# Eight layernorms whose centred residual is made by one product with (identity less 1/128) and read from its PSUM bank

## The reference, cut to what matters

```python
def _layernorm(x, axis=-1, eps=1e-05):
    m = jnp.mean(x, axis=axis, keepdims=True)
    v = jnp.var(x, axis=axis, keepdims=True)
    return (x - m) / jnp.sqrt(v + eps)

    x = L0_attn_x
    x = _layernorm(x + _L0_attn_ref(x, ...), axis=-1)
    x = _layernorm(x + _L0_ffn_ref(x, ...), axis=-1)
...
    x = _layernorm(x + _L3_ffn_ref(x, ...), axis=-1)
    return x
```

## Time and profile before

| | us |
|---|---|
| median of 3 runs | 3070.89 (3068.77 to 3072.56) |
| the profiled execution | 3057.68 |
| its span, first to last instruction | 3055.9 |
| delta rule with its start, 7.4 to 1361.0 | about 1354 |
| one layernorm, first product to last multiply (1361.61 to 1373.91) | 12.3 |

### The profile page before, as it was taken

The page is one execution under the profiler, slowest core; times in us unless marked ns, Lnnn a source line. Parts: engine busy times, 40 slices in busy tenths (PEclk is TensorE's granted clock), DMA queues, the critical chain, the costliest instruction groups (busy, mean ns, idle before and its releaser), DMA issues. The chain is left out here.

```text
span 3055.9 us, 65022 instructions
## 1 busy us (share of the span) xinstructions
PE 2376.6 (78%) x25365; PEld 1619.7 (53%) x25365; DVE 2214.9 (72%) x4056; ACT 1278.8 (42%) x2862; POOL 272.4 (9%) x280
## 2 busy tenths in 40 slices
PE   6677777777777777769947999999767766778677
PEld 5667666666666666643314666666322221222366
DVE  6999999999999999960034877777255657665465
ACT  3333333333333333332225777776411132556334
POOL 0000000000000000000031010100022311110242
PEclk9777787877777878789977999999978887999888
DMA  4111101111111111011018999995000001110421
GB/s 173 30 30 30 30 22 24 30 30 30 30 30 30 30 30 30 16 39 27 0 50 228 250 229 244 234 239 137 35 0 0 0 23 56 41 41 24 156 68 62
DMA packets 200028, 214.43 MB, mean 70 GB/s; under 512 B 32150, under 2 KB 185766, under 8 KB 194310
## 3 DMA queue, kind: packets, MB, share of 16 engines
q1 hardware_dynamic: 197353, 205.39, 25.7%
q0 software_dynamic: 2400, 4.95, 0.5%
HBM read 138.16 MB, written 74.74 MB: 70 GB/s over the span
## 5 line engine op out<-in xcount | busy, mean ns | idle before, releaser
L1274 DVE TENSOR_REDUCE ra_top<-ps 128x1 f32<-128x512 f32 x256 | 161.6, 684 | 96.0 <-PE ps L1078 95.7
L2557 DVE TENSOR_REDUCE dl_ZO<-dl_XP 128x64 f32<-128x128 f32 (+6 forms) x448 | 219.7, 490 | 15.4
L2553 DVE TENSOR_TENSOR dl_XP<-dl_ZO,dl_G 128x64 f32<-128x64 f32 (+6 forms) x448 | 194.6, 434 | 15.4
L1928 DVE TENSOR_TENSOR ps<-ps,da_window 128x192 f32<-128x192 f32 (+1 forms) x256 | 101.3, 396 | 122.3 <-PE ps L1657 117.9
L1772 ACT ACTIVATE da_AB<-ps 128x384 f32<-128x384 f32 x256 | 124.8, 492 | 146.9 <-PE ps L1634 143.2
L1195 ACT ACTIVATE ra_PT<-ps 128x512 f32<-128x512 f32 x256 | 137.0, 597 | 115.6 <-PE ps L1097 115.5
L1782 ACT ACTIVATE da_E<-ps,da_top 128x512 f32<-128x512 f32 x256 | 176.3, 688 | 17.3 <-DVE da_top L1931 16.9
L1931 DVE TENSOR_REDUCE da_top<-ps 128x1 f32<-128x512 f32 x256 | 177.0, 691 | 8.8
L1664 PE MATMUL ps<-ident,da_E 128*128 128x128 f32 x1024 | 169.0, 288 | 1.3 <-ACT da_E L1782 1.2
L1473 POOL MEMSET da_K<- 32x4096 f32 x2 | 7.1, 3574 | 1559.8 <-POOLq L82 1559.8
L2163 PE MATMUL ps<-X,dl_taps_q 128*128 (+1 forms) x1088 | 144.8, 299 | 0.0
(11 more groups left out here) (397 smaller groups left out, 5668.2 us busy)
## 6 DMA issues: line engine op xcount, KB each, us to landing
da_bands<-da_AB SPq DMA_DIRECT2D x128, 384.0 KB, 3.8
dl_Abc<-dl_ends SPq DMA_DIRECT2D x64, 512.0 KB, 6.2
da_window<-da_bands SPq DMA_DIRECT2D x128, 192.0 KB, 4.4
da_across<-da_bands SPq DMA_DIRECT2D x128, 192.0 KB, 4.5
da_parts<-da_split SPq DMA_DIRECT2D x64, 96.0 KB, 3.4
rf_We<-in_rf_We SPq DMA_DIRECT2D x1, 4608.0 KB, 23.2
da_K<-da_parts SPq DMA_DIRECT2D x16, 256.0 KB
da_Q<-da_parts SPq DMA_DIRECT2D x16, 256.0 KB
```

The lines of the kernel that those rows point to most:

```text
L1274: eng.tensor_reduce(top[:, m % 2, u:u + 1], ps[:, score_bank(UNITS * m + u), :], AXX, ALU.max, negate=True).then_inc(s["maxima"], 1)
L2553: link(eng.tensor_tensor(XP[:, :, :, SB - t:], seen.unsqueeze(1).to_broadcast([P, 2, I, t + 1]), G[:, x:x + 2, keys][:, ::-1, :].unsqueeze ...
L2557: link(eng.tensor_reduce(ZO[:, to:to + 1 + (2 * I - 1) * CH:CH].rearrange("p (k i) -> p k i", k=2), XP[:, :, :, SB - 1 - t:], AXX, ALU.add))
```

## The change

Three things are edited.

In the layernorm, a new constant `centre` (the identity less 1/128 in every entry) takes the place of `ones_mean` in the first product, so that bank b holds the centred residual itself. The subtraction L104, its tile `ln_D` and the semaphore `ln_mean` go; the square and the last multiply read bank b. `centre` is loaded in the first block by one more transfer of 64 KB.

In the delta rule, one of the two interleaved copies of the keys is scaled by minus the scale, so that the products come out negative, and plain `beta` is used where `dl_nbeta` was. That takes away the tile `dl_nbeta`, its memset and the instruction L2621, all of them ahead of the loop. The loop has the same instructions as before.

```diff
             eng.dma_start(c.ident[:, :], c.dram["identity"]).then_inc(loaded, 16)
-            eng.wait_ge(loaded, 16 * (B + 1))
+            eng.dma_start(c.centre[:, :], c.dram["centre"]).then_inc(loaded, 16)
+            eng.wait_ge(loaded, 16 * (B + 2))
...
         @block.tensor
         def _(eng):
             for b in range(B):
-                eng.matmul(c.ps[:, b, :], c.ones_mean[:, :], c.R[:, b, :], start=True, stop=True).then_inc(mean, 1)
+                eng.matmul(c.ps[:, b, :], c.centre[:, :], c.R[:, b, :], start=True, stop=True).then_inc(centred, 1)
...
         @block.vector
         def _(eng):
             for b in range(B):
-                eng.wait_ge(mean, base + b + 1)
-                eng.tensor_tensor(D[:, b, :], c.R[:, b, :], c.ps[:, b, :], ALU.subtract).then_inc(centred, 1)
-            for b in range(B):
                 eng.wait_ge(rstd, base + b + 1)
                 eng.wait_ge(centred, base + b + 1)
-                eng.tensor_tensor(c.X[:, b, PAD:PAD + T], D[:, b, :], Q[:, b, :], ALU.mult)
+                eng.tensor_tensor(c.X[:, b, PAD:PAD + T], c.ps[:, b, :], Q[:, b, :], ALU.mult)
...
-                eng.activation(Q[:, b, :], D[:, b, :], ACT.Square).then_inc(squared, 1)
+                eng.activation(Q[:, b, :], c.ps[:, b, :], ACT.Square).then_inc(squared, 1)
...
-                    eng.activation(kqN[:, :, span, 0], kc[:, e, :, :], ACT.Copy, scale=scale)
+                    eng.activation(kqN[:, :, span, 0], kc[:, e, :, :], ACT.Copy, scale=-scale)
...
-            eng.memset(beta[:, T:], 0.0)
-            eng.memset(nbeta[:, T:], 0.0).then_inc(s["prepared"], 1)
+            eng.memset(beta[:, T:], 0.0).then_inc(s["prepared"], 1)
...
             eng.wait_ge(s["beta"], 1)
-            eng.tensor_scalar(nbeta[:, 0:T], beta[:, 0:T], -1.0, None, ALU.mult).then_inc(s["beta"], 1)
-            eng.wait_ge(s["beta"], 2)
```

More of the change, by code:

```diff
@@ L36, in __init__ @@
         self.ident = self.sb("ident", [P, P])
+        self.centre = self.sb("centre", [P, P])
         self.eps = self.sb("eps", [P, 1])
@@ L79, in layernorm @@
     c.norms += 1
-    mean, centred, squared, var, log, rstd = (c.ln[n] for n in (
-        "ln_mean", "ln_centred", "ln_squared", "ln_var", "ln_log", "ln_rstd"))
+    centred, squared, var, log, rstd = (c.ln[n] for n in ("ln_centred", "ln_squared", "ln_var", "ln_log", "ln_rstd"))
     with ExitStack() as ctx:
-        D = c.sb(f"ln_D{base}", [P, B, T], ctx)
         Q = c.sb(f"ln_Q{base}", [P, B, T], ctx)
@@ L2057, in delta_attention @@
         beta = c.sb("dl_beta", [P, T + CP], ctx)
-        nbeta = c.sb("dl_nbeta", [P, T + CP], ctx)
         kc = c.sb("dl_kc", [P, 2, NP, CH], ctx)
@@ L2459, in gate_keys @@
                 eng.wait_ge(s["gt"], 2 * m + 1)
-                ahead = nbeta[:, bass.ds(m * CP, CP)] if not isinstance(m, int) else nbeta[:, m * CP:m * CP + CP]
+                ahead = beta[:, bass.ds(m * CP, CP)] if not isinstance(m, int) else beta[:, m * CP:m * CP + CP]
                 ahead = ahead.rearrange("p (b t) -> p b t", t=SB).unsqueeze(3).to_broadcast([P, CP // SB, SB, SB])
@@ L2481, in prepare @@
                 eng.tensor_tensor(FB[:, e, :, :, :], F[:, e, :, :, 0:SB],
-                                  half_of(nbeta, m, e).rearrange("p (u t) -> p u t", t=SB).unsqueeze(1).to_broadcast([P, I, 2, SB]), ALU.mult)\
+                                  half_of(beta, m, e).rearrange("p (u t) -> p u t", t=SB).unsqueeze(1).to_broadcast([P, I, 2, SB]), ALU.mult)\
                    .then_inc(s["prep"], 1)
@@ L2642, in build @@
         c = Chip(nc, ctx, dram)
-        c.ln = {n: c.sem(n) for n in ("ln_mean", "ln_centred", "ln_squared", "ln_var", "ln_log", "ln_rstd")}
+        c.ln = {n: c.sem(n) for n in ("ln_centred", "ln_squared", "ln_var", "ln_log", "ln_rstd")}
         load_start(c)
@@ L2683, in laid_out @@
         "xT": g["L0_attn_x"].transpose(2, 0, 1),
-        "identity": np.eye(P, dtype=np.float32),
+        "identity": np.eye(P, dtype=np.float32), "centre": np.eye(P, dtype=np.float32) - np.float32(1.0 / P),
         "tf_w1": g[L0 + "w1_w"].T, "tf_w2": g[L0 + "w2_w"].T, "tf_h1": rows_in(g[L0 + "h1_w"].T),
```

## The result

| | before | after |
|---|---|---|
| median, us | 3069.99 (3064.12 to 3072.56, 6 runs) | 3176.09 (3161.69 to 3187.72, 6 runs) |
| the profiled execution | 3057.68 | 3187.72 |
| its span | 3055.9 | 3185.9 |
| ratio of the runs | | 1.0343 [1.0312, 1.0374] |

The forecast was 3070.3 in a range of 3066 to 3076. The time is 106 us away from it, so something cost a hundred times what the terms of the sum were about.

What follows compares the result with a forecast made beforehand. PE's sixteen passes were taken to bound each layernorm up to the last logarithm, then exponentials and multiplies; loads bound the start. Multiplies -0.8 and the `centre` load +0.2 sum to -0.6 us: from 3070.89 to 3070.3, range 3066 to 3076.

Steps and rivals of the forecast that it cites:

- Same instructions, another sign. Value 0.: Delta-rule loop: the moved minus sign leaves its instructions the same and costs or gains nothing.
- The section on `dl_nbeta`: Start of the delta rule: removing L2621 (0.46 us) and the memset (about 0.05) is hidden by waits; value 0, at best -0.46.
- Rival D: Delta loop: tiles and instructions lying elsewhere change VectorE's times, 5 ns each, about 12 us, 3082 or 3058; chance 5%.
- Rival C: Layernorm openings: one more or fewer at PE's half clock, 2.9 us, giving 3073.2 or 3067.4; chance 9%, half each way.
- The subtractions: Layernorms: the 32 removed VectorE subtractions, 22.0 us busy, lie beside PE's passes, so removing them is worth 0.
- rival A: Layernorms: the subtraction was on the path, so each loses 0.73 us, 5.8 in all, giving 3064.5; chance 4%.
- The square from PSUM: Layernorms: ScalarE's square reading PSUM takes about 598 ns and keeps up with PE; the last logarithm stays put; value 0.
- The multiplies: Layernorm tail: four VectorE multiplies reading PSUM take 2.40 us against 2.50, -0.10 per layernorm, -0.8 us for eight.
- Rival B: Layernorm tail: PSUM reads slow VectorE's multiplies, up to +0.50 per layernorm, +4.5 us with the later load, 3075.4; chance 10%.
- The load of `centre`: First block: the extra 64 KB transfer ahead of the first wait is paid in full, +0.2 us, up to +0.47.
- `dl_nbeta` in the start: Start of the delta rule: VectorE's wait before turning the key products grows from 1.39 to about 1.9 us; value 0.
- The condition named for being wrong: The prediction fails if PE waits for a square anywhere, or the 55 to 1361 us stretch changes by over 1 us.

Runs made afterwards that it cites:

- pad1: The kernel after plus one memset of one column on VectorE in the first block, so its loop begins at 195: 3071.56 us, 1.0 against before.
- slot0: The kernel after with the head of VectorE's delta-rule loop placed by an alignment directive: 3069.39 us, 0.9994 against before.
- pad2: The kernel after plus two memsets of one column on VectorE in the first block, so its loop begins at 196: 3067.93 us, 0.9994 against before.
- hint: The kernel after plus one instruction at the top of each loop turn announcing the closing branch: 3071.72 us, 0.9993 against before.
- before_minus2: The kernel before with two memsets moved from VectorE to GpSimd, so its loop, still 264 long, begins at 194: 3175.31 us, 1.0328.

## Why the prediction was wrong

**The step that failed is one sentence: "Same instructions, another sign. Value 0."** Two things were wrong with it. It isn't the same instructions: the loop has 262 in place of 264. And the value of a loop was taken from its instructions alone, while its place in VectorE's code has a price too. The section on `dl_nbeta` made the same slip a line above: it priced L2621 and the memset by what they take to run (0.46 and 0.05 us, hidden) and not by what it means that two instructions ahead of the loop are gone. The runs put +104.5 us there (after less pad1), two hundred times the largest price considered for it. Pad1 shows that one instruction in the place of the two lost ones was enough.

**Rival D was the right place with the wrong mechanism and size.** It asked whether the delta loop runs otherwise "because its tiles and instructions lie elsewhere", but spread a made-up 5 ns over 2411 instructions, 3082 or 3058, and dismissed it because instructions of one shape take the same time on different tiles. They do. The loss isn't in any instruction's duration, but in one gap per turn. The row that could have raised the chance was on the page of before, unused: the code queue's packets, 51 for the whole run, with only 4 in the 1200 us of a loop of 15 turns. That says that the loop is held by a memory, hence that it could fail to be. How near the edge it stood (196 against 195) no row of before shows; an honest chance for it would have been larger than 5% and its price tens of us, but not most of the probability.

**Rival C moved, within its price.** Before, the fifth and the seventh layernorm open slowly, with 6.55 and 5.68 us for eight passes; after, only the fifth does, with 6.53, and all others take 3.67. One fewer is 2.0 us less in this profile. Over the twelve profiles it is one to three of the eight, in slow kernels and in quick ones, so it doesn't explain the 106 us.

**The subtractions: right, and rival A did not happen.** Value 0, as L98's 15.4 us in 64 pieces and the chain show.

**The square from PSUM: right.** Predicted 598 ns, measured 597; it starts with the end of the table load (1475.96), and the first logarithm came at 4.56 us after the first pass, with the last where it was.

**The multiplies: mis-sized.** The term was -0.10 each, -0.8 in all. Measured was 2.48 against 2.50 us for four, so -0.02 each and -0.2 in all. I had taken L1268's 2.40 us, whose operands come from PSUM in the same way, but nothing there has to wait for ScalarE. Here the last multiply starts 1484.51 + 2.48 - 0.68 = 1486.31, just behind the last exponential (1483.85 + 2.19 = 1486.04): the exponentials, at 0.55 us each, set the pace. Rival B, the dearer PSUM read, did not happen: one multiply takes 684 ns with a PSUM source and took 688 without.

**The load of `centre`: in the upper part of its range.** The second block's first load was issued at 7.73 against 7.43, so +0.30, where I took 0.2 and gave 0.47 as the end. VectorE's first instruction on taps came at 20.20 against 19.70, 0.50 later, about one more issue (0.47):

```profile
7.73 0.33 SPq L136 DMA_DIRECT2D dl_Wb<-in_dl_Wb  x1
...
20.20 4.42 DVE L2613 TENSOR_TENSOR dl_taps_v<-dl_taps_v,dl_G 128x4096 f32<-128x4096 f32 x1 [8.77 <-DMA dl_taps_v<-in_dl_cw]
...
52.29 2.32 DVE L2454 STREAM_TRANSPOSE dl_G<-ps 128x2048 f32<-128x2048 f32 x1 [2.47 <-PE ps L2170]
```

**`dl_nbeta` in the start: direction right.** The wait before the turning of the key products grew from 1.39 to 2.47 us, more than the 1.9 foretold, since TensorE's products of the keys came 1.1 us later (52.29 against 51.19). 0.49 of that is the loads' delay, which reaches TensorE's first projection (24.68 against 24.19). The other 0.61 is that projection itself: its 64 products (L2159 after, L2163 before) took 9.65 us against 9.04, with a granted clock of 0.89 against 0.95 in 20 to 52 us, after TensorE had stood idle 4.89 us for the taps and not 2.77. It is paid once.

**Sum of what was priced.** With the loop's place mended, the change is worth nothing that can be measured: pad1 1.0 [0.999, 1.0009], slot0 0.9994 [0.9984, 1.0005]. The terms but the one that failed come to the forecast of 3070 within the noise, which also hides that the multiplies and the start were each off by some tenths of a us.

The condition named for being wrong ("the stretch from 55 to 1361 us changes its length by more than 1 us") was the one that came true. No version beats the kernel before clearly: pad2, slot0 and hint lie 0.06 to 0.07% under it, and all three intervals contain 1.

## What to carry to other kernels

An instruction that is removed ahead of a long loop moves the loop in its engine's code. Count the loop's instructions and where it begins, and look at the packets of the code queues within the loop: none per turn means held, some per turn means loaded again. How many pieces the loop touches can be counted only once an edge is known; here the edges were found by moving the loop an instruction at a time, and only on VectorE. In a profile the sign is a wait by "issue" at the first instruction of a loop's body, once per turn; one spare instruction ahead of the loop or a hint for the closing branch cured it here. And before a difference is given to an edit, cut the span at marks that both profiles have, since a part that no edit touched (here the routed one, 193.8 against 205 to 210 us) can differ by more than the edit is worth.

## What the runs showed of the hardware that I had not expected

- VectorE's code is loaded in packets of 8.2 KB, and the edges lie 128 instructions apart: 194 slow and 195 quick at one end, 451 slow and 450 quick at the other, 322 slow.
- A loop of 262 or 264 instructions over four pieces stops for 6.1 to 7.9 us per turn at its top in the mean (78.8 us in 13 turns in before_minus2, 102.4 in after; the longest stops are 7.0 and 8.9), though all five packets of a turn together are only 0.04 MB. What sets the price of a packet, and why the two kernels differ, stays open.
- A hint for the closing branch does not only bring the load forward. It took away all the loads of a turn, 67 packets down to 3 in 100 to 1300 us.
- VectorE's stop is passed on whole: TensorE's idle time that ends with VectorE's `dl_W` is now 196.1 us before L2191, against 75.5 before the same products in the kernel before (L2195), and the time from 188 to 276 us has 60.73 us of TensorE's work where before has 68.86. Before, then after:

```profile
L2195 PE MATMUL ps<-ident,dl_W 128*128 128x128 f32 x128 | 29.6, 375 | 75.5 <-DVE dl_W L2547 75.5
...
L2191 PE MATMUL ps<-ident,dl_W 128*128 128x128 f32 x128 | 34.3, 422 | 196.1 <-DVE dl_W L2543 196.1
```
